# Two windowed-attention layers on one core: row maxima and their subtraction over half a step, a new order of the stages on every engine, and ScalarE's table loads written ahead of the waits

## The reference, cut to what matters

```python
xn   = layernorm(x) * g1 + b1                  # over 48 channels
q,k,v = split(windows(xn) @ wqkv + bqkv)        # windows of 7 x 7 = 49 tokens, 6 heads of 8
attn = softmax(q @ k.T * 8**-0.5 + bias[+mask]) # 49 x 49 for each window and head
x    = x + unwindow((attn @ v) @ wp + bp)
x    = x + gelu(layernorm(x) * g2 + b2 @ w1 + c1) @ w2 + c2
```

## Time and profile before

| | before |
|---|---|
| median of 3 runs | 5472.18 us |
| profiled execution | 5478.46 us, span 5476.5 us |
| PE busy | 5300.4 us (97%) |
| DVE busy | 4225.1 us (77%) |
| ACT busy | 3998.4 us (73%) |
| POOL busy | 3597.7 us (66%) |
| chain that ended last | PE 93% |

### The profile page before, as it was taken

The page is one execution under the profiler, slowest core; times in us unless marked ns, Lnnn a source line. Parts: engine busy times, 40 slices in busy tenths (PEclk is TensorE's granted clock), DMA queues, the critical chain, the costliest instruction groups (busy, mean ns, idle before and its releaser), DMA issues.

```text
span 5476.5 us, 249903 instructions
## 1 busy us (share of the span) xinstructions
PE 5300.4 (97%) x102530; PEld 3552.8 (65%) x102530; DVE 4225.1 (77%) x7241; ACT 3998.4 (73%) x6155; POOL 3597.7 (66%) x3737
## 2 busy tenths in 40 slices
PE   6699999999999999999999999999999999999987
PEld 3466666666666666666666666666666666666655
DVE  6678787887888777777777777877887878778864
ACT  0177777777777778777778787877787777777760
POOL 4477766766767666666666666677776677676740
PEclk7599999999999999999999999999999999999995
DMA  7311111111111111111111111111111111111119
GB/s 226 119 31 29 31 29 29 31 29 29 31 29 31 29 29 31 29 31 28 30 29 31 29 29 31 29 30 30 29 32 29 29 31 29 29 31 29 31 53 273
DMA packets 288443, 238.91 MB, mean 44 GB/s; under 512 B 43576, under 2 KB 282906, under 8 KB 287002
## 3 DMA queue, kind: packets, MB, share of 16 engines
q1 hardware_dynamic: 246802, 179.90, 12.4%
q0 software_dynamic: 8192, 22.49, 1.2%
q10 hardware_dynamic: 32282, 20.03, 1.2%
HBM read 112.93 MB, written 109.36 MB: 41 GB/s over the span
## 4 chain that ended last, share of the span: by engine, by line
PE 93%; DMA 4%; issue 1%; DVE 1%; SPq 0%; POOL 0%; ACT 0%; DVEq 0%; ACTq 0%; POOLq 0%
PE pB L1091 10%; PE pA L1103 10%; PE pB L1079 10%; PE pS L1067 10%; PE pS L1113 6%; PE pA L1079 6%; PE pS L1040 5%; PE pA L1134 5%; PE pS L1155 5%; PE pS L1079 4%; PE pA L1055 4%; PE pS L1165 3%; PE pS L1145 3%; PE pB L1017 3%; PE pA L1017 3%; PE pB L1009 2%
## 5 line engine op out<-in xcount | busy, mean ns | idle before, releaser
L463 POOL TENSOR_TENSOR S<-S,mx 113x588 f32<-113x588 f32 x1536 | 1786.1, 1185 | 21.9 <-DVE mx L810 21.9
L797 DVE TENSOR_TENSOR S<-pS,bias 113x588 f32<-113x588 f32 x1536 | 1113.0, 767 | 819.7 <-PE pS L1067 819.7
L449 POOL TENSOR_TENSOR Kbd<-KT,headmask 128x588 f32<-128x588 f32 x768 | 896.1, 1167 | 1094.4 <-DVE KT L819 1094.4
L810 DVE TENSOR_REDUCE mx<-S 113x12 f32<-113x588 f32 x1536 | 1126.4, 754 | 0.1
L493 POOL TENSOR_TENSOR xn<-x,rs 112x392 f32<-112x392 f32 x384 | 390.9, 1018 | 450.6 <-ACT rs L566 450.5
L555 ACT ACTIVATE sq<-pB 112x392 f32<-112x392 f32 x384 | 190.9, 497 | 657.6 <-PE pB L1009 657.6
L1079 PE MATMUL pB<-ident,S 113*113 113x113 f32 x4608 | 620.5, 271 | 0.3
L838 DVE COPY V<-pA 49x192 f32<-49x192 f32 x1536 | 545.5, 355 | 72.0 <-PE pA L1055 4.8
L1091 PE MATMUL pB<-E,V 113*32 113x98 f32 x18432 | 597.6, 248 | 0.8 <-issue 0.8
L1067 PEld LDWEIGHTS pS<-Kbd,Qt 24*49 24x49 f32 x24576 | 355.6, 117 | 368.9 <-issue 368.9
L1103 PE MATMUL pA<-E,keyones 113*32 113x392 f32 x4608 | 593.1, 503 | 1.8 <-ACT va L559 1.7
(11 more groups left out here) (134 smaller groups left out, 8875.3 us busy)
## 6 DMA issues: line engine op xcount, KB each, us to landing
xin<-xT SPq DMA_DIRECT2D x384, 98.0 KB, 2.0
xT<-xout SPq DMA_DIRECT2D x384, 98.0 KB, 1.9
xin<-xT SPq DMA_DIRECT2D x384, 73.5 KB, 2.0
xT<-xout SPq DMA_DIRECT2D x384, 73.5 KB, 1.8
xT<-cm POOLq DMA_DIRECT2D x128, 171.5 KB, 3.8
cm<-xT SPq DMA_DIRECT2D x128, 171.5 KB, 3.4
tm<-in_x SPq DMA_DIRECT2D x128, 147.0 KB
out<-tm ACTq DMA_DIRECT2D x128, 147.0 KB
```

The costliest lines, as they stand in the source:

```text
L449: return pool.tensor_tensor(y, x, m, ALU.mult)
L463: pool.tensor_tensor(s, s, m, ALU.subtract).then_inc(sub_done[half][wh], 1)
L797: dve.tensor_tensor(strided(S[:, b, w, 0, 0, 0:1], [[KEYS, 2], [2 * KEYS, 2 * HP], [1, N]]), strided(pS[0:M2, 2 * wh, 0:1], [[512, 2], [N, ...
L810: dve.tensor_reduce(m, s, AX.X, ALU.max).then_inc(mx_done[half][wh], 1)
```

## The change

1. `maxima` and `less_maximum` handle a half step (2 x 588 elements in each partition) in one instruction, where they handled a quarter (588) in each of two. One semaphore replaces two, so `turn_scores` of either quarter waits for the subtraction of both.
2. The order of the stages is new on PE, DVE, ACT and POOL, and so are the pairs in `HOME` and the bank waits that follow from them. SP stores step s5 where it stored s4.
3. `gelu_table` is an explicit load ahead of `hidden_c`'s waits, and `normal_table` stands ahead of `exponentials(s3, 1, 1)` where it stood behind `hidden_ab`. It is still two loads in a step. `attend` and `sums` wait for the exponentials of quarter 11 and no longer of 10.

The core of the diff:

```diff
-        HOME = dict(ctr1=3, var1=3, qk=1, value=2, attend=3, sums=2, project=0, ctr2=0, var2=2, up=2, upc=0, down=1, turn00=2, turn01=3, turn10=3, turn11=1)
+        HOME = dict(ctr1=2, var1=3, qk=2, value=1, attend=2, sums=2, project=3, ctr2=0, var2=3, up=0, upc=1, down=3, turn00=1, turn01=0, turn10=3, turn11=2)
...
-            def less_maximum(j, half, wh):
+            def less_maximum(j, half):
...
-                s = strided(S[:, b, w, 0, 0, 0:1], [[KEYS, 4 * HP], [1, N]])
-                m = strided(mx[:, b, w, 0, 0:1], [[1, 4 * HP], [0, N]])
-                pool.tensor_tensor(s, s, m, ALU.subtract).then_inc(sub_done[half][wh], 1)
+                s = strided(S[:, b, w, 0, 0, 0:1], [[J * 2 * HP * KEYS, 2], [KEYS, 4 * HP], [1, N]])
+                m = strided(mx[:, b, w, 0, 0:1], [[J * 2 * HP, 2], [1, 4 * HP], [0, N]])
+                pool.tensor_tensor(s, s, m, ALU.subtract).then_inc(sub_done[half], 1)
...
+            def gelu_table(j):
+                act.preload_act_table_set(PH[j.t]["table_set"])
...
-            LATEST = [(1, 0)]
+            LATEST = [(1, 1)]
```

More of the change, by code:

```diff
@@ L231, in build @@
         s_mm = [sem(f"s_mm{h}") for h in range(2)]
-        bias_done, mx_done, sub_done, turn_mm, exp_done = (
+        bias_done, turn_mm, exp_done = (
             [[sem(f"{n}{h}{wh}") for wh in range(2)] for h in range(2)]
-            for n in ("bias_done", "mx_done", "sub_done", "turn_mm", "exp_done"))
+            for n in ("bias_done", "turn_mm", "exp_done"))
+        mx_done, sub_done = ([sem(f"{n}{h}") for h in range(2)] for n in ("mx_done", "sub_done"))
         pv_mm, sums_mm = sem("pv_mm"), sem("sums_mm")
@@ L405, in iteration @@
                     load(s0.next())
-                if s4:
-                    store(s4)
+                if s5:
+                    store(s5)
             sweep(sp, iteration)
@@ L644, in iteration @@
                     log_sums(s3)
+                if s4:
+                    log_var2(s4)
+                if s4:
+                    inverse_std2(s4)
                 if s3:
                     inverse_sums(s3)
[L647 to L651, removed]
             sweep(act, iteration)
@@ L800, in add_bias, with maxima @@
                    .then_inc(bias_done[half][wh], 1)
-            def maxima(j, half, wh):
+            def maxima(j, half):
                 b = j.mod(2)
-                w = J * wh + 2 * half
-                dve.wait_ge(bias_done[half][wh], gv(j, 1, 1))
+                w = 2 * half
+                for wh in range(2):
+                    dve.wait_ge(bias_done[half][wh], gv(j, 1, 1))
                 if not j.before(2):
[L807 to L810, removed]
+                    dve.wait_ge(sub_done[half], gv(j, 1, -1))
+                s = strided(S[:, b, w, 0, 0, 0:1], [[J * 2 * HP * KEYS, 2], [KEYS, 4 * HP], [1, N]])
+                m = strided(mx[:, b, w, 0, 0:1], [[J * 2 * HP, 2], [1, 4 * HP]])
+                dve.tensor_reduce(m, s, AX.X, ALU.max).then_inc(mx_done[half], 1)
             def evac_k(j):
@@ L885, in iteration @@
             def iteration(s0, s1, s2, s3, s4, s5, s6):
+                if s1:
+                    maxima(s1, 0)
+                if s1:
+                    evac_va(s1)
+                if s1:
+                    evac_vb(s1)
+                if s1:
+                    add_bias(s1, 1, 1)
+                if s1:
+                    add_bias(s1, 1, 0)
+                if s3:
+                    normal_o(s3)
+                if s1:
+                    maxima(s1, 1)
                 if s0:
@@ L1179, in iteration @@
                     elif s1:
                         pe.wait_ge(va1_done, gv(s1, 1, 1))
-                    center1(s0)
-                if s4:
+                    elif s3:
+                        pe.wait_ge(exp_done[1][0], gv(s3, 1, 1))
+                    project(s4)
+                if s1:
+                    if s5:
+                        pe.wait_ge(hAB_done, gv(s5, 1, 1))
+                    elif s2:
+                        pe.wait_ge(exp_done[0][1], gv(s2, 1, 1))
+                    if s5:
+                        pe.wait_ge(hC_done, gv(s5, 1, 1))
+                    elif s2:
+                        pe.wait_ge(exp_done[0][0], gv(s2, 1, 1))
+                    scores(s1, 0)
@@ L1185, in iteration @@
+                if s4:
+                    if s1:
+                        pe.wait_ge(bias_done[0][0], gv(s1, 1, 1))
+                    elif s5:
+                        pe.wait_ge(hAB_done, gv(s5, 1, 1))
+                    elif s2:
+                        pe.wait_ge(exp_done[0][1], gv(s2, 1, 1))
+                    center2(s4)
+                if s1:
+                    if s1:
+                        pe.wait_ge(bias_done[0][1], gv(s1, 1, 1))
                     elif s5:
@@ L1187, in iteration @@
                     elif s2:
-                        pe.wait_ge(bias_done[1][0], gv(s2, 1, 1))
-                    center2(s4)
-                if s3:
[L1191 to L1200, removed]
+                        pe.wait_ge(exp_done[0][0], gv(s2, 1, 1))
@@ new lines, in iteration @@
+                    value(s1)
+                if s0:
+                    if s2:
+                        pe.wait_ge(exp_done[1][0], gv(s2, 1, 1))
+                    elif s4:
+                        pe.wait_ge(x1_done, gv(s4, 1, 1))
+                    elif s6:
+                        pe.wait_ge(x2_done, gv(s6, 1, 1))
+                    elif s5:
+                        pe.wait_ge(va2_done, gv(s5, 1, 1))
+                    elif s1:
+                        pe.wait_ge(va1_done, gv(s1, 1, 1))
+                    var1(s0)
```

279 lines of the change are left out of this document (118 added, 161 removed).

## The result

| | before | after |
|---|---|---|
| median | 5474.04 us (5471.5 to 5478.05, 4 runs) | 5601.51 us (5595.94 to 5603.84, 4 runs) |
| ratio, 95% interval | | 1.0229 [1.0214, 1.0245] |
| one step of PE, median of 383 | 13.02 us | 13.28 us |

A forecast was written before the change was run, and what follows sets the result against it. PE, busy 97% and never waiting in steady state, bounds the kernel. Its work of 13.01 us plus waits of 0.21 and 0.05 makes a 13.27 us step, 95 us more over some 378 steps: 5567 us, range 5515 to 5605.

The forecast's parts named there:

- PE sets the time; the merging and the loads are hidden: Only PE's stream counts; merged maxima and subtractions on DVE and POOL, and SP's later store, were costed at nothing.
- PE's own work, 13.01: PE's step without waits: prices for changes of tile shape between neighbouring groups sum to -0.01 us, from 13.02.
- the wait of `scores` 0: PE waits at `scores` 0 for ACT's `hAB`: 1.31 us against 1.26 of PE work, wait 0.05.
- the wait of `var1`: PE waits at `var1` for the exponential of quarter 10: 0.16 us, or 0.21 with the price of entering.
- The three waits: New PE waits: `var1` for exponential 10, 0.16 us; `scores` 0 for `hAB`, 0.05; `value` for DVE's additions, 0.02.
- the prediction's own sign: In the profile after, `var1` following `value` without an idle mark would show the forecast wrong; about 0.15 us was expected.
- The round closes, step 13.27: The delay at `var1` holds up `up`, `hAB`, `scores` 0, transposes and exponentials in turn: 13.01 + 0.21 + 0.05 us.
- ACT's run ties with PE's: From `hAB`'s start to the exponentials, ACT takes 2.62 us with overlap, PE 2.62; without overlap ACT takes 2.72.
- 95 us: Whole kernel: 0.25 us more a step over some 378 steps; 5573 us profiled, 5567 median after taking off 6.
- Loop branches, 0 with 20 on either side: At six places where the loop goes back, PE stood 2.95 us; change taken as 0, with 20 us either side.
- Draining loads: Rival, chance 0.01: behind ACT's second table load the exponential starts 1.38 us later; step 14.65, time 6090 us.
- Faster, since `project` pays nothing on leaving: Rival, chance 0.06: PE's `project` costs 0.72 instead of 0.82 and no wait shows; step 12.91, 5430 us.

The follow-up runs named there:

- run 1: Kernel after with maxima and subtractions cut into quarters again, everything else as after: 5607.83 us, ratio 1.0244 to the kernel before.
- run 2: Kernel before with only the maxima and subtractions merged: 5476.27 us, ratio 1.0002 to the kernel before.
- run 3: Kernel after with GELU replaced by the square and both table loads taken out: 5593.72 us, ratio 1.0218 to the kernel before.
- run 5: Kernel before with only the GELU table loaded explicitly ahead of `hidden_c`'s waits: 5476.68 us, ratio 1.0004 to the kernel before.
- one_block_v: Another stage order against the kernel before, worked out with corrected DVE copies: four transposes in one block, `value` behind `down_c`; 5310.98 us, ratio 0.969.
- Run 4: Kernel after with four `HOME` entries changed and bank waits following, so `var1` waits for exponential 11: 5569.55 us, ratio 1.0171 to the kernel before.
- pairs: Kernel before with the pairs of `up` and `up_c` exchanged and one `ready()` gone, PE's order unchanged: 5459.06 us, ratio 0.9968.
- one_block: A new stage order against the kernel before: four transposes in one block, `value` with `query_key`, quarters kept; 5423.53 us, ratio 0.9899.

## Why the prediction was right, point by point

- **PE sets the time; the merging and the loads are hidden.** Right. Runs 1, 2, 3 and 5 each changed one of them and left the step at 13.28 or 13.02. PE's busy share did not fall by two points as announced; it stayed at 97%, since the waits vanish in the overlap.
- **PE's own work, 13.01.** Right in most of its parts: the groups of after stand at their prices within 0.02, but for `project`, 0.86 with the wait of `scores` 0 in it, and `value`, 0.53 with the wait of `var1` in it. That `value` alone is 0.37 is shown by `one_block_v`. That `project` alone is 0.82 isn't shown by any run: `scores` 0 starts 0.15 behind `hAB` whatever `project` costs, as long as that is under 0.86. For the same reason an error in this price would have done no harm: what it took from PE's work it would have given to the wait.
- **The three waits.** `var1` 0.16 (0.53 - 0.37), `scores` 0 0.04 if `project` is 0.82 (priced 0.05), `value` 0.01 to 0.02 (priced 0.02), each at its releaser's end plus 0.15. Run 4 took the first away and with it 32 us, where some 80 were expected of that in the simple form. By the prediction's own sign it would have been wrong, since `var1` follows `value` without an idle mark; the sign was badly chosen. The wait is shown by the lag: `value`'s row (2714.36 + 0.63 = 2714.99) still overlaps `var1`'s start at 2714.89, so a wait of this size leaves no mark.
- **The round closes, step 13.27.** Right: 13.275. That ACT's run ties with PE's held too: the two end within 0.01 of each other (2713.46 and 2713.45), and run 3 shows that shortening ACT's side alone gives nothing. PE's side alone was not shortened in any run.
- **95 us.** The steady part measured 98.8 (0.258 a step where 0.25 was priced, over 383 steps where 378 were).
- **Loop branches, 0 with 20 on either side.** The branches gave +5. The mis-sized term is another one: the prediction had none for isolated long steps, and 94 in place of 62 gave most of the 22 us, the ends 5 more. Of the 34 us by which 5601.5 stands above 5567, these are 27; the step gave 4 more than priced, and the last 4 are that the profiled execution of after lies only 2.3 us above its median, where the prediction took off 6.
- **Draining loads.** The rival fell. Behind the second load the exponential starts 0.03 after its end (2712.18 + 1.28 = 2713.46, start 2713.49), and removing both loads changed the step by 0.00.
- **Faster, since `project` pays nothing on leaving.** Fell: the waits are there and the step is 13.28. What `project` pays on leaving is hidden behind the wait.

Left open is what makes a step long now and then. That it depends on PE's no-ops and bank waits is shown by `pairs` (two pairs exchanged and one `ready()` less, 24 us less excess); the missing `ready()` is not enough by itself, as the kernel after lacks it too and has 94 long steps. That some gaps are at equal distances and carry no semaphore doesn't say what they are, and no run here tells it apart.

## What to carry to other kernels

When one engine is busy for 97% and waits for nothing, the first things worth moving are its neighbours: write down what each group costs between which neighbours, and count the changes of tile shape before trying an order. 12 changes against 12 promised nothing, and then every wait of a tenth is a loss; 9 changes gave 3% where PE waited for nothing, and 1% in `one_block`, where it did. And read waits by laying the end of the releaser plus the usual lag beside the start of the waiting group, since short ones leave no mark. Count every instruction of the other engines in such a working: two copies forgotten on DVE, busy for 77%, cost most of the expected gain (55 us came of 195).

## What the hardware showed that I had not expected

- Behind each of the six loop branches the granted clock fell to 0.50 (1.2 of 2.4 GHz) for a while, in the kernel before and after. The length of the stop alone doesn't say for how long: before, 3.28 us at 4736 left an average of 0.91 in the 20 us around it and 2.99 us at 2513 one of 0.74; after, 3.29 us at 1391 left 0.83 and 3.31 us at 846 left 0.66.
- Exchanging two PSUM pairs between two groups that wait for nothing, with one no-op of PE's less, gave 0.3% through fewer isolated gaps, with a median step equal to the nanosecond.
- Removing 2.57 us of table loads a step from an engine that PE waits for in each step gave nothing in the step.
